# A soft clamp's reciprocal moved from ScalarE's Ln and Exp to VectorE's reciprocal, in a four-layer perceiver kernel

## What is computed

```
q, k = mh_rmsnorm(q), mh_rmsnorm(k)          # 16 query heads, 8 key heads, head size 64
sim  = einsum('bhgid,bhjd->bhgij', q, k)
sim  = tanh(sim / 50) * 50 * 64 ** -0.5
attn = softmax(where(causal, -max, sim))     # 32 x 32 scores for each batch and head
x    = x + (attn @ v) @ Wout
```

## Time and profile before

| | |
|---|---|
| median of three runs | 6848.6 us (6839.22 to 6852.55) |
| the profiled execution | 6848.6 us |
| its span, first to last instruction | 6846.8 us |
| mean granted TensorE clock | 0.752 |
| busy: TensorE matmul, VectorE, ScalarE, GpSimd | 5107.7, 3026.2, 1934.5, 659.6 us |

### The profile page before, as it was taken

How to read it: one execution, slowest core, us unless ns; L and a number is a source line. 1 busy time by engine, 2 the same in 40 slices (tenths; PEclk the granted TensorE clock), 3 DMA queues, 4 the chain that set the end, 5 groups by cost and what they waited for, 6 DMA issues and landing times.

```text
span 6846.8 us, 94942 instructions
## 1 busy us (share of the span) xinstructions
PE 5107.7 (75%) x32012; PEld 3672.0 (54%) x32012; DVE 3026.2 (44%) x8343; ACT 1934.5 (28%) x5131; POOL 659.6 (10%) x438
## 2 busy tenths in 40 slices
PE   5768687687876868768787686866778668786777
PEld 4545555465555655555555464544655446555455
DVE  3445335353454534445344443445434454444543
ACT  3223222232323313223132331423313233232331
POOL 1101011010110102001020010200002000020000
PEclk8759687696876968669686696867868678685887
DMA  3000100001000010000100001000000000000000
GB/s 118 1 1 1 35 7 1 1 1 38 4 1 1 1 38 5 1 1 1 38 4 1 1 1 39 3 1 1 13 27 3 1 1 13 27 3 1 1 1 2
DMA packets 17466, 74.76 MB, mean 11 GB/s; under 512 B 2106, under 2 KB 10298, under 8 KB 10436
## 3 DMA queue, kind: packets, MB, share of 16 engines
q1 hardware_dynamic: 16964, 68.29, 3.0%
HBM read 66.18 MB, written 2.10 MB: 10 GB/s over the span
## 4 chain that ended last, share of the span: by engine, by line
issue 82%; POOL 9%; PE 6%; DVE 2%; ACT 1%; POOLq 0%; DVEq 0%; ACTq 0%
POOL own L1203 3%; POOL big L1203 2%; POOL odd L1220 2%; POOL mid L1203 2%; POOL own L1208 1%; PE dveb L401 1%; PE actb L863 1%; PE oddb L873 0%; PE evenb L554 0%; PE evenb L685 0%; PE dveb L704 0%; PE oddb L554 0%; PE evenb L608 0%; PE oddb L677 0%; PE evenb L654 0%
## 5 line engine op out<-in xcount | busy, mean ns | idle before, releaser
L1203 POOL TENSOR_TENSOR own<-own,rinv 128x1028 f32<-128x1028 f32 x128 | 243.1, 1899 | 2918.9 <-DVE rinv L1669 2918.9
L935 ACT ACTIVATE lnv<-mv,wts 128x2 f32<-128x2 f32 x257 | 75.9, 295 | 1467.7 <-DVE mv L1355 1425.4
L393 PE MATMUL actb<-wts,xn 128*128 128x128 f32 x418 | 118.1, 385 | 487.3 <-DVE xn L1361 232.4
L942 ACT ACTIVATE PT<-actb 128x512 f32<-128x512 f32 (+2 forms) x576 | 313.5, 578 | 423.0 <-PE actb L469 143.8
L685 PE MATMUL evenb<-ctxT,big 128*128 128x257 f32 x1024 | 284.7, 402 | 127.4 <-ACT own L1105 115.3
L1105 ACT ACTIVATE own<-evenb,nmax 128x257 f32<-128x257 f32 x512 | 238.8, 472 | 417.8 <-DVE nmax L1655 417.8
L393 PEld LDWEIGHTS actb<-wts,xn 128*128 128x128 f32 x418 | 59.2, 187 | 543.6 <-issue 484.5
L1460 DVE CUSTOM_DVE_ANT_0 big<-evenb,own 128x257 f32<-128x257 f32 x512 | 198.6, 421 | 302.1 <-issue 301.5
L704 PE MATMUL dveb<-PT,ctx 128*128 128x512 f32 x512 | 260.2, 632 | 60.1 <-ACT PT L942 60.1
L685 PEld LDWEIGHTS evenb<-ctxT,big 128*128 128x128 f32 x1024 | 178.1, 194 | 234.2 <-ACT own L1105 166.4
L436 PE MATMUL evenb<-big 32*128 32x257 f32 x1024 | 238.2, 502 | 56.0 <-DVE nmax L1460 40.3
(11 more groups left out here) (350 smaller groups left out, 11468.4 us busy)
## 6 DMA issues: line engine op xcount, KB each, us to landing
ctxT<-in_ctxT SPq DMA_DIRECT2D x16, 1032.0 KB, 4.6
own<-in_fside SPq DMA_DIRECT2D x64, 257.0 KB, 7.7
ctx<-in_ctx SPq DMA_DIRECT2D x16, 1024.0 KB, 6.8
wts<-in_weights SPq DMA_DIRECT2D x1, 10592.0 KB
big<-in_fold SPq DMA_DIRECT2D x1, 2048.0 KB, 8.6
x<-in_x SPq DMA_DIRECT2D x16, 128.0 KB, 2.5
out<-xn SPq DMA_DIRECT2D x16, 128.0 KB, 1.9
mid<-in_ints SPq DMA_DIRECT2D x1, 576.0 KB
```

What stands on the lines that cost most here:

```text
L393: last = transpose(ps[:, 128 * t:128 * t + 128], xn[s][:, t, :], ident)
L942: op = activation(dst, ps[0:parts, 0:n], func or ACT.Copy, scale=scale)
L1203: nc.gpsimd.tensor_tensor(P[:, :, 0:SK], P[:, :, 0:SK], rinv[0][:, :].unsqueeze(2).to_broadcast((128, 4, SK)), ALU.mult).then_inc(*p_ready ...
```

## The change

ScalarE's Ln and second Exp are taken out. After the first Exp has drained `evenb`, VectorE adds 1 and takes a reciprocal, both in place on `Sm[s]`, and raises `s_ready`; ScalarE waits for it in stage 8 and applies the last Exp. VectorE's two instructions are in stage 8 as well, ahead of its stage 9. The rest of the diff keeps count of the semaphores.

```
-    sq_ready=0, act_step=40, bias_ready=2, ctxm_ready=2, dve_step=196, ...
+    sq_ready=0, act_step=36, bias_ready=2, ctxm_ready=2, dve_step=198, ...
-    ... s_ready0=4, s_ready1=4, ...
+    ... s_ready0=5, s_ready1=5, ...
@@ ScalarE, a1p
                     activation(Sm[s].rearrange("p (t c) -> p t c", t=TG), evenb[:, :, :], ACT.Exp, scale=2.0 / 50.0).then_inc(*eR.drained.both())
-
-                    def step(op):
-                        op.then_inc(*act_step.done)
-                        act.wait_ge(*act_step.at(trip, act_step.count))
-
-                    act.wait_ge(*eR.drained.at(trip, eR.keys[(s, k, ("s", 1))]))
-                    step(activation(Sm[s], Sm[s], ACT.Ln, bias=w("ones128")[:, 0:1]))
-                    step(activation(Sm[s], Sm[s], ACT.Exp, scale=-1.0))
+                    yield
+                    act.wait_ge(*s_ready[s].next("ACT", trip))
                     activation(Sm[s], Sm[s], ACT.Exp, scale=-2.0 * 50.0 / 8.0).then_inc(*e_ready[s].done)
-                    yield
                     yield
@@ VectorE, a1p
                     yield
+                    dve.wait_ge(*eR.drained.at(trip, eR.keys[(s, k, ("s", 1))]))
+                    then(V.tensor_scalar(Sm[s], Sm[s], 1.0, None, ALU.add))
+                    V.reciprocal(Sm[s], Sm[s]).then_inc(*s_ready[s].done)
                     yield
                     dve.wait_ge(*e_ready[s].next("DVE", trip))
```

More of the change, by code:

```diff
@@ L43 @@
 PER_TRIP = dict(
-    sq_ready=0, act_step=40, bias_ready=2, ctxm_ready=2, dve_step=196, inv_ready=32, logs_ready=2, rope_out=20,
+    sq_ready=0, act_step=36, bias_ready=2, ctxm_ready=2, dve_step=198, inv_ready=32, logs_ready=2, rope_out=20,
     rq_ready=4, ss_ready=4, x0_exp=16, x2_min=64, x3_exp=4, x3_min=4, ctx_free0=1, ctx_free1=1, own_free0=1,
     own_free1=1, y_ready0=1, y_ready1=1, var_ready0=16, var_ready1=16, rstd_ready0=16, rstd_ready1=16,
-    xn_ready0=13, xn_ready1=13, s_ready0=4, s_ready1=4, e_ready0=6, e_ready1=6, p_ready0=21, p_ready1=21,
+    xn_ready0=13, xn_ready1=13, s_ready0=5, s_ready1=5, e_ready0=6, e_ready1=6, p_ready0=21, p_ready1=21,
     mix_ready0=10, mix_ready1=10, act_bank_filled=208, act_bank_drained=208, dve_bank_filled=160,
```

## The result

The changed kernel takes 7033.9 us in the median of four runs (7029.5 to 7041.1), the kernel before 6849.7 us, now in the median of four: a ratio of 1.0267, with a 95% interval of 1.0246 to 1.0289. It is 184 us slower. The forecast was 91 us slower.

The account below looks back on a forecast made before the run. It took ScalarE's chain to set the pace with stream 0 in the attention and VectorE with stream 1. Shifts of 39.9 + 51.1 = 91.0 us on 6848.6 gave 6940 us, 1.3% slower, range 6912 to 6972.

Parts of the forecast that it names:

- What bounds the place: At the changed lines, ScalarE's chain sets the pace with stream 0 in attention, VectorE with stream 1.
- case 1: Stream 0 in the attention: mask's multiply and L642 shift 4.99 us later, eight times, 39.9 us.
- case 2: Stream 1 in the attention: VectorE's experts' work L1639 and TensorE's L642 come 6.39 us later, eight times, 51.1 us.
- The reciprocal: New VectorE instruction on 128 x 1024: 6.25 ns a column from the shorter rows, 6553 ns, taken as 6.55 us.
- The add: New VectorE add of 1 on 128 x 1024: 637 ns by 0.46 ns a column, at most 1226 ns.
- The two stalls: Delays of L642 in the two attention cases, 4.99 and 6.39 us, eight times each, 91.0 us together.
- Case 2 is absorbed: Rival: VectorE's delay with stream 1 in attention is recovered further on, leaving 39.9 us, 6889 us; chance 0.04.
- every rival with another reciprocal: Two rivals: cheap on a long row, 6845 us at 0.64 us, chance 0.02; dearer, 8150 ns, 6965 us, chance 0.04.
- the likeliest case: Both stalls in full, 6940 us, chance 0.77; spans 6926 to 6968 with upper bounds of add and reciprocal.
- The clock: TensorE's granted clock elsewhere: uncertain by 12 us either way, half the spread between two trips, over eight trips.
- the longer stall can't lower it there: After both stalls TensorE's granted clock is already 0.50, the lower level, 1.2 GHz, so no added cost there.
- the clock costs more: Rival: longer idle TensorE rises later to the higher level, one L677 step per case, 27 us, 6967 us; chance 0.11.

Follow-up runs that it names:

- the second profile: Profile of the changed kernel run once more with no edit; measured 7036.8 us, 1.0264, span of the profile 7017.6 us.
- The Tanh kernel: Kernel before, with ScalarE's Tanh and one Exp in place of Exp, Ln and Exp, plus table loads; 6882.8 us, 1.0051.
- the one with three repeats: Kernel before, with stream 0's mask multiply repeated three more times, changing no values; +29 us, 1.0044.
- the two cases alone: Kernel before with the change applied only in stream 0 (6946.7 us, 1.0130), or only in stream 1 (6941.9 us, 1.0125).

## Why the prediction was wrong

- **What bounds the place, right.** In case 1 ScalarE's chain was awaited, in case 2 VectorE's. L573's wait grew to 8.74 us (forecast 8.7), and L1635 starts 7.24 us after the first Exp ends (forecast 7.3).
- **The reciprocal, right.** 6553 ns, the very value of the line through 32 and 256 columns. The prediction's estimate from the Trainium skill (page "VectorE: DVE Perf Modes", section "First, the fixed hardware budget"), which read the repeat count of 8 as 8 cycles a column, was 8.15 us; the trace disagrees with that reading. **The add**, 694 ns, was forecast at 637; 16 times 57 ns is 1 us.
- **The two stalls, right.** 5.06 and 6.23 us against 4.99 and 6.39; 90 us against 91. "Case 2 is absorbed" was wrong, and so was every rival with another reciprocal. The lower edge of the likeliest case should read 6928 by its own terms, not 6926; nothing hangs on it.
- **The clock, wrong; this step failed.** The prediction held that "the longer stall can't lower it there". That is so behind L642, which takes 3.67 us in both kernels; the L677 within case 2's stall was lowered, at no cost. It sized what the clock does elsewhere at 12 us either way, from the spread of two trips of the kernel before, and this is the term that failed: it measured 94 and 89 us with the changed kernel, and from -5 to +97 us over the table. The rival "the clock costs more" named the right sign, but behind the stalls and at 27 us. What the runs show: a displacement of one to some twelve us a trip, by any means, can change in which stretches TensorE is granted 2.4 GHz, from right behind it to hundreds of us away. The kernel before falls well in the two stretches above, though not in layer 3. The spread between trips of one kernel was therefore the wrong row to size it from. In the first profile of the changed kernel the trips repeat the same clock, so that the loss is multiplied by eight. The first Exps of stream 0 in trips 2 to 4, beside the earlier trace rows, are 856.42 and 856.75 us apart, not 852.6:

```profile
1271.71 1.02 ACT L1070 ACTIVATE own<-evenb 128x1024 f32<-128x1024 f32 x1 [6.44 <-PE evenb L629]
...
2128.13 1.02 ACT L1070 ACTIVATE own<-evenb 128x1024 f32<-128x1024 f32 x1 [6.44 <-PE evenb L629]
...
2984.88 1.02 ACT L1070 ACTIVATE own<-evenb 128x1024 f32<-128x1024 f32 x1 [6.44 <-PE evenb L629]
```

In the second profile they are not alike, and longer: 863.49 and 863.26 us here, from 860.1 to 867.0 over all trips. The same three:

```profile
1267.13 1.02 ACT L1070 ACTIVATE own<-evenb 128x1024 f32<-128x1024 f32 x1 [6.45 <-PE evenb L629]
...
2130.62 1.02 ACT L1070 ACTIVATE own<-evenb 128x1024 f32<-128x1024 f32 x1 [6.44 <-PE evenb L629]
...
2993.88 1.02 ACT L1070 ACTIVATE own<-evenb 128x1024 f32<-128x1024 f32 x1 [6.45 <-PE evenb L629]
```

The lengths of the trips also speak for theory B. The Tanh kernel and the one with three repeats differ by 5.7 us of work a trip, and yet the last four trips of both take 846.5 us each. By the sum of their work they would differ.

Shown: the extra lies in stretches without a changed line, where TensorE's same matmuls take longer at a lower granted clock; it comes with a displacement alone; it doesn't grow with the displacement's size. How the 94 us of the timed executions divide over stretches no profile shows: the two of the changed kernel hold 37 and some 80 us. Argued only: that the cause is the position of the work against the moments at which the clock is set. The near additivity of the two cases alone, 173 of 179, would then be chance. Open: what selects the clock of layer 3, in which two executions of one program differ, and which displacement falls well.

The Trainium skill says on the page "TensorE: Matmul & The Clock Gate", section "Part 1: The HAM clock gate (the "warmup" mystery)", that how many matmuls run slow at a kernel's start varies from run to run, and that for modelling this ramp costs less than 1% of a typical kernel's span. This kernel goes between the two levels throughout (mean granted clock 0.752 before), so the page's figure for the start doesn't bound the clock's part here: the rest reaches 97 us, 1.4% of the span. That executions of one program differ, the two profiles of the changed kernel show for the whole kernel (0.740 and 0.734).

## What to carry to other kernels

A reciprocal on VectorE costs 6.25 ns a column, more than Ln and Exp on ScalarE together (2.2 us for 1024 columns against 6.55), so it doesn't pay on whole score tiles. In a kernel like this one, whose TensorE is granted either level about half of the time, a forecast from rows gives the mechanical part; the clock's part must be put in the range at its full size, here some 100 us upward from a baseline that falls well. Before a change of under 2% is blamed or praised, the same kernel should be run with a small neutral delay or two: a result that flips with 1.3 us more work a trip is the clock's.

## What was not expected of the hardware

One program (the reciprocal on 256 columns) took 6864 us in one execution and 6950 us in another, at a mean granted clock of 0.747 and 0.730, with all its instructions the same. And 2.5 us a trip of added work took some 30 us off what the changed kernel costs over the kernel before.
